# Mamba layer with routed experts on one core: the last state of batches 1 to 5 scaled by ScalarE behind the transposes, y in two parts

## The chip, the cores and the metric

One core of a Trainium2 chip. The metric is device time in microseconds of one execution. The engines are called by their names; in rows of the profile PE is TensorE, DVE is VectorE, ACT is ScalarE, POOL is GpSimd and SP is SyncE.

## The reference

x is 8 batches of 512 tokens of 128 features. After a layer norm (xn), two branches are added to x. The first is a Mamba block with 256 inner channels and 16 states:

```python
x_s, z = split(rmsnorm(xn) * norm_w @ in_proj_w.T)
u = silu(depthwise_conv4(x_s) + conv_b)
dt_raw, B, C = split(u @ x_proj_w.T)
delta = softplus(dt_raw @ dt_proj_w.T + dt_proj_b)
dA = exp(delta * A);  dBu = delta * u * B
h = dA_t * h + dBu_t            # over the 512 tokens, for each channel and state
y_t = sum over the 16 states of h * C_t
out = ((y + u * D) * silu(z)) @ out_proj_w.T + xn
```

The second routes each of the 4096 tokens to 2 of 8 experts (a gated FFN of inner width 352) and adds their weighted outputs.

## The kernel before, in words

The work goes by 8 batches b and, in each, by 16 states k; a pair is a step, numbered n = 16 b + k. Channels lie on partitions in two halves (hf = 0, 1), the 512 tokens along the free dimension, so one instruction handles 128 x 512 elements. Five engines run own instruction streams, each written out by hand in a function `step(b, k)` (`step0(k)` for batch 0), and they are tied by counting semaphores. There is no planner: what stands first in an engine's stream is done first.

One step in batches 1 to 5:
- ScalarE writes exp(delta * A_k) into a PSUM bank for each half (`decay_bank`, L554); two banks alternate.
- GpSimd computes dBu for both halves (`scaled`, L996) into one of two buffers; it may start when the scan two steps back has ended. It also issues the indirect loads of token rows (`load`, L980) and, spread over a batch, 11 elementwise products for the next batch's delta and gate.
- VectorE scans the tokens (`scan`, L1213) in place in the bank, then multiplies by C's row, which a DMA has spread over the partitions, into `h_sb` (`product`, L1232).
- TensorE transposes `h_sb` in 8 blocks of 128 x 128 and adds them up in PSUM banks 2 and 3 (`accumulate`, L1507), tokens now on partitions. The banks so hold the sum over the states.

State 0 of batches 1 to 5 is done otherwise (`BY_SCALAR`): the scan writes `h_sb` directly, there is no product, and ScalarE multiplies the transposed state in place in banks 2 and 3 by C's column (`multiplied`, L744: one value a partition, four copies of 128 x 256). It must be alone in the banks for that, so it is the first of a batch.

The end of a batch: after the transposes of state 15, ScalarE copies both banks to `y_sb` (`y_evac`, L761, in step 0 of the next batch), TensorE transposes this back with 8 transposes into the same banks (`y_turn`, L1603; they are called YB then), and VectorE multiplies by the gate (`gate`, L1240) into `g_sb`, which shares its memory with `y_sb`. Only then may state 0 of the next batch be transposed into the banks.

The 72 tiles of 128 routed tokens are laid over the steps from (1, 4) to (5, 11), one a step, in the gaps of all engines. In step g with tile j: TensorE does the down matmuls of tile j - 1 (L1672), the up matmuls of j (L1686), the gate matmuls of j + 1 (L1680) and the transpose of the rows of j + 2 (L1664). ScalarE does the output of j - 1 (`out_out`, L787), tanh of j + 1 (`gate_out`, L780) and the xT copy of j + 2 (`slots_out`, L769). VectorE does two products (L1259, L1266); the second waits for the up matmuls. Ahead of one another in TensorE's stream in step 0 of a batch stand: transposes of state 15, down, up, `y_turn`, gate matmuls, rows transpose, `rows` of a later batch (L1556), transposes of state 0; in step 1 down and up follow.

Batch 0 computes the routing beside its steps: `logits` (L1425), `choices` on VectorE, `totals` and `ranking` on TensorE with `totals_out` (L496) and `ranks_out` on ScalarE between them, one-hots on VectorE and `inverse` (L1455) on TensorE, and `sources` on VectorE (L1176 to L1181), from which GpSimd's loads take their indices. `keep` (L1411) is a matmul without use for its result. `by_vector` and `bank_read` translate "state m is done" into the semaphore and count to wait for:

```python
BY_SCALAR = [S * b for b in range(1, NB - 2)]
def by_vector(m):
    return m - sum(min(max(m - 2 * n, 0), 2) for n in BY_SCALAR)
def bank_read(eng, m):
    if m > 0 and (m - 1) // 2 in BY_SCALAR:
        wait(eng, "h_rdy", m)
    else:
        wait(eng, "p_rdy", by_vector(m))
```

## Time and profile before

| | |
|---|---|
| median of 3 runs | 606.79 us (605.84 to 608.28) |
| profiled execution, its own time | 606.02 us |
| its span, first to last instruction | 604.2 us |
| TensorE | 535.1 us busy, 3578 matmuls |
| VectorE | 581.3 us busy |
| ScalarE | 465.9 us busy |
| GpSimd | 489.8 us busy |
| mean granted TensorE clock | 0.980 |

The sum is made against the execution that the profile shows, 606.02 us. A row of a timeline is: start, duration, engine, line, operation, output and inputs, count of instructions merged, and in brackets the idle time before it with what ended it. Durations of merged rows are from the first start to the last end; the next group may start about 0.1 us before that. Step 0 of batch 3 begins with the scan at 262.53 us.

### The profile page before, as it was taken

The numbers are of one execution on the slowest core, as the hardware profiler recorded it, in microseconds if no ns is written. First come the engines' busy times: TensorE is split into PE (matmuls) and PEld (weight loads), VectorE is DVE, ScalarE is ACT, GpSimd is POOL, SyncE is SP. The second block draws the span as 40 slices with busy tenths as digits, with TensorE's granted clock in tenths as the row PEclk, the third lists the DMA queues.
The fourth block names the chain that finished last, engine by engine and source line by source line (L and its number), as shares of the span: only waits on it lengthen the run. The fifth ranks groups of instructions, "written<-read, shape, count | busy, mean of one in ns | idle before, by whom it ended". The sixth has DMA issues, their size and how long they took to land.

```text
span 604.2 us, 11465 instructions
## 1 busy us (share of the span) xinstructions
PE 535.1 (89%) x3578; PEld 419.5 (69%) x3578; DVE 581.3 (96%) x841; ACT 465.9 (77%) x952; POOL 489.8 (81%) x383
## 2 busy tenths in 40 slices
PE   5899889898898998999989999899989697778887
PEld 2377766647787878877887778877777465656564
DVE  6999989989999999999999999999999998999997
ACT  3899696369957998579876798768995589969880
POOL 3793466479999899998999889998997967885784
PEclk9899798989999999999999999999999999989999
DMA  7320229625787887889768888778874455233374
GB/s 200 148 91 2 74 60 282 226 84 184 237 314 237 311 277 222 292 244 339 262 189 305 276 305 275 243 257 274 284 264 157 156 219 197 103 100 108 79 143 87
DMA packets 61038, 122.48 MB, mean 203 GB/s; under 512 B 8362, under 2 KB 41778, under 8 KB 53938
## 3 DMA queue, kind: packets, MB, share of 16 engines
q1 hardware_dynamic: 53826, 112.42, 55.1%
q0 software_dynamic: 6144, 9.00, 6.6%
q10 hardware_dynamic: 1008, 0.33, 0.3%
q8 instruction: 29, 0.48, 0.3%
q14 instruction: 31, 0.25, 0.1%
HBM read 112.25 MB, written 9.47 MB: 201 GB/s over the span
## 4 chain that ended last, share of the span: by engine, by line
POOL 34%; PE 26%; DVE 15%; issue 14%; ACT 10%; DMA 1%; ACTq 0%; DVEq 0%; POOLq 0%; SPq 0%
POOL dbu L996 18%; POOL xs L980 6%; DVE bank L1213 6%; DVE h_sb L1232 5%; PE bank L1507 4%; PE bank L1541 3%; PE bank L1672 3%; ACT dbu L570 3%; PE bank L1686 2%; PE bank L1556 2%; ACT da L542 2%; PE bank L1564 2%; PE bank L1680 2%; POOL delta L463 2%; POOL sp_m L448 2%
## 5 line engine op out<-in xcount | busy, mean ns | idle before, releaser
L996 POOL TENSOR_TENSOR dbu<-du,xn_all 128x1024 f32<-128x1024 f32 x86 | 203.6, 2368 | 22.3 <-DVE bank L1213 13.7
L1213 DVE TENSOR_TENSOR_SCAN bank<-bank,dbu 128x512 f32<-128x512 f32 x160 | 195.2, 1222 | 1.0 <-ACT bank L554 0.7
L1232 DVE TENSOR_TENSOR h_sb<-bank,xh_all 128x512 f32<-128x512 f32 x230 | 152.5, 677 | 1.0
L1507 PE MATMUL bank<-id_sb,h_sb 128*128 128x128 f32 x992 | 132.5, 277 | 11.8 <-DVE h_sb L1232 9.3
L554 ACT ACTIVATE bank<-delta,a_sb 128x512 f32<-128x512 f32 x170 | 117.1, 691 | 27.5 <-DVE h_sb L1232 22.8
L1507 PEld LDWEIGHTS bank<-id_sb,h_sb 128*128 128x128 f32 x992 | 112.5, 143 | 26.5 <-DVE h_sb L1232 14.5
L1213 DVE TENSOR_TENSOR_SCAN bank<-da,bank 128x512 f32<-128x512 f32 x82 | 96.1, 1213 | 4.0 <-PE bank L1468 3.2
L1672 PEld LDWEIGHTS bank<-wd_sb,hid 117*128 117x128 f32 (+1 forms) x432 | 55.4, 190 | 42.8 <-issue 26.3
L980 POOL DMA_INDIRECT xs<-xn_rows,src x72 | 70.4, 978 | 12.8 <-issue 9.5
L1672 PE MATMUL bank<-wd_sb,hid 117*128 117x128 f32 (+1 forms) x432 | 62.9, 281 | 17.9 <-ACT xT L769 17.9
L570 ACT ACTIVATE dbu<-du_t,bc_sb 128x256 f32<-128x256 f32 x164 | 69.4, 497 | 5.8 <-PE bank L1468 3.4
L1468 PE MATMUL bank<-id_sb,dbu 128*128 128x128 f32 x328 | 51.6, 282 | 16.5 <-DVE h_sb L1232 9.1
L1541 PE MATMUL bank<-xhT,wk_sb 128*128 128x512 f32 x128 | 62.6, 617 | 1.4 <-ACT sp_m L866 0.8
L1468 PEld LDWEIGHTS bank<-id_sb,dbu 128*128 128x128 f32 x328 | 38.0, 144 | 37.2 <-issue 23.7
L542 ACT ACTIVATE da<-delta,a_sb 128x512 f32<-128x512 f32 x86 | 58.1, 713 | 4.8 <-DVE bank L1213 4.7
L1680 PE MATMUL bank<-xT,wgu_sb 128*118 128x128 f32 x432 | 59.0, 273 | 0.3 <-DVE ga L1259 0.3
L1686 PE MATMUL bank<-xT,wgu_sb 128*118 128x128 f32 x432 | 59.0, 272 | 0.0
L780 ACT ACTIVATE th<-bank 118x384 f32<-118x384 f32 x72 | 35.0, 485 | 29.1 <-PE bank L1680 28.3
L1046 POOL DMA_INDIRECT xhT<-y_slots,slot x40 | 38.7, 967 | 17.9 <-DVE bank L1213 7.1
L1686 PEld LDWEIGHTS bank<-xT,wgu_sb 128*118 128x118 f32 x432 | 52.7, 181 | 0.5 <-issue 0.5
L1680 PEld LDWEIGHTS bank<-xT,wgu_sb 128*118 128x118 f32 x432 | 52.4, 182 | 0.5 <-issue 0.5
L787 ACT ACTIVATE ys<-bank,stat 128x128 f32<-128x128 f32 x72 | 26.4, 366 | 24.8 <-PE bank L1672 24.3
(205 smaller groups left out, 906.8 us busy)
## 6 DMA issues: line engine op xcount, KB each, us to landing
xh_all<-b_rows SPq DMA_DIRECT2D x30, 1024.0 KB
xn_all<-b_rows SPq DMA_DIRECT2D x25, 1024.0 KB
wgu_sb<-in_w_gu SPq DMA_DIRECT2D x72, 352.0 KB, 4.2
wd_sb<-in_w_dn SPq DMA_DIRECT2D x72, 192.0 KB, 5.8
y_slots<-ys SPq DMA_DIRECT2D x72, 64.0 KB
xn_rows<-xn_all SPq DMA_DIRECT2D x2, 1040.0 KB, 10.2
out<-x_sb SPq DMA_DIRECT2D x7, 256.0 KB, 7.2
x_sb<-in_x SPq DMA_DIRECT2D x2, 640.0 KB, 5.9
```

The costliest lines, as they stand in the source:

```text
L554: nc.scalar.activation(bank_of(b, m)[:, :], delta[b % 2][:, hf, :], ACT.Exp, scale=a_sb[:, hf, k:k + 1]).then_inc(s["da_rdy"], 1)
L570: last = nc.scalar.activation(dbuT[k % 2][:, t, :], duT[:, t, :], ACT.Copy, scale=bc_sb[q][:, t, k:k + 1])
L980: nc.gpsimd.indirect_dma_start(xs[i][:, :], None, xn_rows, bass.IndirectOffsetOnAxis(ap=src[:, j:j + 1], axis=0)).then_inc(s[f"xs_in{i}"], 16)
L996: nc.gpsimd.tensor_tensor(dbu[k % 2][:, :, :], du[b % 2][:, :, :], b_ring[c % 2][:, k % CH, :].unsqueeze(1).to_broadcast([P, NH, T]), ALU. ...
L1213: nc.vector.tensor_tensor_scan(to, da_of(n)[:, hf, :] if n in IN_SBUF else at, inp, 0.0, ALU.mult, ALU.add).then_inc(s["h_rdy"], 1)
L1232: nc.vector.tensor_tensor(h_sb[k % 2][:, hf, :], bank_of(b, 2 * k + hf)[:, :], row, ALU.mult).then_inc(s["p_rdy"], 1)
L1468: last = nc.tensor.transpose(at[:, t * P:(t + 1) * P], dbuT[k % 2][:, t, hf * P:(hf + 1) * P], id_sb[:, :])
L1507: last = MM(HT[i][:, t % 2, hf * P:(hf + 1) * P], h_sb[k % 2][:, hf, t * P:(t + 1) * P], id_sb[:, :], is_transpose=True, start=(k == 0 and ...
L1541: last = MM(at[:, :], wk_sb[:, tap, hf * P:(hf + 1) * P], xhT[:, c, tap:tap + T], start=(tap == taps[0] if c == 0 else tap == 0), stop=(ta ...
L1672: last = MM(XD[:, P:P + H], hid[j % 2][0:FN[c], c * P:(c + 1) * P], wd_sb[j % NW][0:FN[c], c, :], start=(c == 0), stop=(c == NF - 1))
L1680: last = MM(GB[0:FW, c * P:(c + 1) * P], wgu_sb[j % NW][:, c * FS:c * FS + FW], xT[j % 2][:, :], start=True, stop=True)
L1686: last = MM(UB[0:FW, c * P:(c + 1) * P], wgu_sb[j % NW][:, F + c * FS:F + c * FS + FW], xT[j % 2][:, :], start=True, stop=True)
```

## The change

For batches 1 to 5 state 15 is treated like state 0: scan into `h_sb`, no product on VectorE. Since its C column is another than that of the sum in the banks, the sum of states 0 to 14 is first copied out by ScalarE (`summed_out`, in step 15), then the transposes of state 15 are written to the banks afresh (`start` set), and ScalarE copies them out with the scale of C's column (`spread`, four copies, in step 0 of the next batch). y so lies in two buffers (`da[1]`, `da[2]`, idle in batches 1 to 5), and `y_turn` adds both with 16 transposes. The gate waits for its half of y only. `own_columns` copies all 16 columns of C. In batch 0, the logits of batches 4 and 5 move one step later each (3 to 4, 4 to 5), one `keep` falls away, `totals_out` moves ahead of `vanishing(1, 1)` on ScalarE, y of batch 0 is turned ahead of `inverse(6)`, and `sources` moves from the end of step (1, 0) into step (1, 1), behind its first scan.

```diff
@@ near L152
+        parts_of = {b: [by_time(v) for v in ((da[1], da[2], da[0]) if b < 6 else (sp_m, sp_y, sp_e))] for b in range(NB - 1)}
+
+        def y_at(b):
+
+            if b in TRAILING:
+                return parts_of[b][0:1 + len(TRAILING[b])]
+            return [y_end if b == NB - 1 else parts_of[b][0] if 0 < b < 5 else y_sb]
+
+        def y_count(b):
+
+            return 2 * sum(len(y_at(b0)) for b0 in range(b))
@@ near L222
-        LOGITS_AT = {1: (3,), 3: (4,), 4: (5,), 6: (6, 7)}
+        LOGITS_AT = {1: (3,), 4: (4,), 5: (5,), 6: (6, 7)}
@@ near L241
-        BY_SCALAR = [S * b for b in range(1, NB - 2)]
+        LEADING = [S * b for b in range(1, NB - 2)]
+        TRAILING = {b: (S - 1,) for b in range(1, 6)}
+        BY_SCALAR = sorted(LEADING + [S * b + k for b, ks in TRAILING.items() for k in ks])
@@ ScalarE, step0
                 if k in (7, 8):
                     magnitudes(1, k - 7)
+                    if k == 8:
+                        totals_out()
                     vanishing(1, k - 7)
                 if k == 8:
-                    totals_out()
                     own_columns(1)
@@ ScalarE, step
-                if g - 1 in BY_SCALAR:
+                if 0 < b < 6:
+                    trailing(b, k)
+                if g - 1 in LEADING:
                     rows(b + 1)
                     multiplied(g - 1)
@@ ScalarE
-                nc.scalar.activation(bc_sb[c % 2][:, :, S:S + 1], at[:, 2 * P:3 * P].rearrange("p (t c) -> p t c", t=TT)[:, :, S:S + 1],
+                nc.scalar.activation(bc_sb[c % 2][:, :, S:2 * S], at[:, 2 * P:3 * P].rearrange("p (t c) -> p t c", t=TT)[:, :, S:2 * S],
                                      ACT.Copy).then_inc(s["cc_rdy"], 1)

             def y_evac(b):

+                if b in TRAILING:
+                    spread(b, S - 1)
+                    return
                 last = (b + 1) * S if b < NB - 1 else (NB - 1) * S + TURNED + 1
+                summed_out(last, y_at(b)[0])
+
+            def summed_out(last, at):
+
                 for i in range(2):
                     wait(act, "acc_mm", 2 * last - 1 + i)
-                    at = y_sb if b < NB - 1 else y_end
                     nc.scalar.activation(at[:, 2 * i:2 * i + 2, :], HT[i], ACT.Copy).then_inc(s["y_out"], 1)
+
+            def spread(b, k):
...
+                for i in range(2):
+                    act.wait_ge(s["acc_mm"], 2 * n + i + 1)
+                    for t in (2 * i, 2 * i + 1):
+                        last = nc.scalar.activation(at[:, t, :], HT[i][:, t % 2, :], ACT.Copy,
+                                                    scale=bc_sb[b % 2][:, t, S + k:S + k + 1])
+                    last.then_inc(s["y_out"], 1)
+
+            def trailing(b, k):
+
+                ks = TRAILING.get(b, ())
+                if k in ks and k == ks[0]:
...
+                    summed_out(b * S + k, y_at(b)[0])
@@ VectorE
             def gate(b):

                 wait(dve, "o_mm", b)
-                dve.wait_ge(s["yb_mm"], 2 * b + 2)
                 dve.wait_ge(s["z_rdy"], 2 * b + 2)
                 for hf in range(NH):
+                    dve.wait_ge(s["yb_mm"], 2 * b + (hf + 1 if b in TRAILING or 0 < b < 5 else 2))
@@ VectorE, step
+                if b == 1 and k == 1:
+                    sources()
                 product(b, k, 0)
...
-                if b == 1 and k == 0:
-                    sources()
@@ TensorE, accumulate
                 for i in range(2):
-                    if n - 1 in BY_SCALAR:
-                        pe.wait_ge(s["hc_rdy"], 2 * BY_SCALAR.index(n - 1) + i + 1)
+                    if n - 1 in LEADING:
+                        pe.wait_ge(s["hc_rdy"], 2 * LEADING.index(n - 1) + i + 1)
+                    if k in ks:
+                        pe.wait_ge(s["y_out"], y_count(b) + 2 * ks.index(k) + i + 1)
                     for t in (2 * i, 2 * i + 1):
                         for hf in range(NH):
                             last = MM(HT[i][:, t % 2, hf * P:(hf + 1) * P], h_sb[k % 2][:, hf, t * P:(t + 1) * P], id_sb[:, :],
-                                      is_transpose=True, start=(k == 0 and t % 2 == 0 and hf == 0), stop=(k == S - 1),
+                                      is_transpose=True, start=((k == 0 or k in ks) and t % 2 == 0 and hf == 0),
+                                      stop=(k == S - 1 or k + 1 in ks),
                                       skip_group_check=True)
@@ TensorE, y_turn
-                pe.wait_ge(s["y_out"], 2 * b + 2)
-                at = y_sb if b < NB - 1 else y_end
+                pe.wait_ge(s["y_out"], y_count(b + 1))
                 for hf in range(NH):
                     for t in range(TT):
-                        last = MM(YB[hf][:, t * P:(t + 1) * P], at[:, t, hf * P:(hf + 1) * P], id_sb[:, :], is_transpose=True,
-                                  start=(t == 0), stop=(b < NB - 1), skip_group_check=True)
+                        for i, at in enumerate(y_at(b)):
+                            last = MM(YB[hf][:, t * P:(t + 1) * P], at[:, t, hf * P:(hf + 1) * P], id_sb[:, :], is_transpose=True,
+                                      start=(t == 0 and i == 0), stop=(b < NB - 1 and i == len(y_at(b)) - 1), skip_group_check=True)
@@ TensorE, step0
-                if k in (0, 4):
+                if k == 0:
                     keep(LGB[:, 2 * C - 2 * H + 2 * E:])
@@ TensorE, step
                 if k == 0:
                     accumulate(g - 1)
                     if b == 1:
+                        y_turn(0)
                         inverse(6)
                         inverse(7)
...
-                if g in BY_SCALAR:
+                if g in LEADING and b > 1:
                     y_turn(b - 1)
```

How ScalarE's stream changes from step 15 of batch 1 to step 0 of batch 2 (the other middle batches are alike). Before, from the output of tile j - 1 in step 15 (`ys`; `bank<-delta` are the decays, `th` is tanh, `xT` the copy, `g_sb` the evacuation of y; the name ahead of a bracket is the semaphore waited for):

```order
L787 ACTIVATE ys<-bank,stat 128x128 [waits wt_rdy,ys_out0,dn_mm]
L554 ACTIVATE bank<-delta,a_sb 128x512 [waits delta_rdy,p_rdy]
L780 ACTIVATE th<-bank 118x384 [waits ga_rdy,g_mm]
L769 ACTIVATE xT<-bank 128x128 [waits u_mm,xt_mm]
L773 ACTIVATE stat<-xs,stat 128x1
L554 ACTIVATE bank<-delta,a_sb 128x512 [waits delta_rdy,p_rdy]
L761 ACTIVATE g_sb<-bank 128x512 [waits acc_mm] x2
L787 ACTIVATE ys<-bank,stat 128x128 [waits wt_rdy,ys_out1,dn_mm]
```

The same place in the changed kernel, whose line numbers differ:

```order
L785 ACTIVATE da<-bank 128x512 [waits acc_mm] x2
L836 ACTIVATE ys<-bank,stat 128x128 [waits wt_rdy,ys_out0,dn_mm]
L567 ACTIVATE bank<-delta,a_sb 128x512 [waits delta_rdy,h_rdy]
L829 ACTIVATE th<-bank 118x384 [waits ga_rdy,g_mm]
L818 ACTIVATE xT<-bank 128x128 [waits u_mm,xt_mm]
L822 ACTIVATE stat<-xs,stat 128x1
L567 ACTIVATE bank<-delta,a_sb 128x512 [waits delta_rdy,h_rdy]
L798 ACTIVATE da<-bank,bc_sb 128x256 [waits acc_mm,cc_rdy]
L798 ACTIVATE da<-bank,bc_sb 128x256
L798 ACTIVATE da<-bank,bc_sb 128x256 [waits acc_mm]
```

Two copies that wait for TensorE's transposes now stand ahead of everything else in step 15, and four copies stand where two stood.

TensorE's stream at the start of step 0 of batch 2, before (transposes of state 15, down, up, y, gate):

```order
L1507 MATMUL bank<-id_sb,h_sb 128x128 [waits p_rdy]
L1507 MATMUL bank<-id_sb,h_sb 128x128 x7
L1672 MATMUL bank<-wd_sb,hid 128x128 [waits xt_rdy,ys_rdy,hid_rdy]
L1672 MATMUL bank<-wd_sb,hid 128x128 x2
L1686 MATMUL bank<-xT,wgu_sb 118x128 [waits hid_rdy]
L1686 MATMUL bank<-xT,wgu_sb 118x128 x2
L1603 MATMUL bank<-id_sb,g_sb 128x128 [waits y_out]
L1603 MATMUL bank<-id_sb,g_sb 128x128 x7
L1680 MATMUL bank<-xT,wgu_sb 118x128 [waits ga_rdy,w_in1,xt_rdy]
```

And with the change:

```order
L1559 MATMUL bank<-id_sb,h_sb 128x128 [waits y_out,h_rdy]
L1559 MATMUL bank<-id_sb,h_sb 128x128 x3
L1559 MATMUL bank<-id_sb,h_sb 128x128 [waits y_out]
L1559 MATMUL bank<-id_sb,h_sb 128x128 x3
L1725 MATMUL bank<-wd_sb,hid 128x128 [waits xt_rdy,ys_rdy,hid_rdy]
L1725 MATMUL bank<-wd_sb,hid 128x128 x2
L1739 MATMUL bank<-xT,wgu_sb 118x128 [waits hid_rdy]
L1739 MATMUL bank<-xT,wgu_sb 118x128 x2
L1656 MATMUL bank<-id_sb,da 128x128 [waits y_out]
L1656 MATMUL bank<-id_sb,da 128x128 x15
L1733 MATMUL bank<-xT,wgu_sb 118x128 [waits ga_rdy,w_in1,xt_rdy]
```

The transposes of state 15 wait for ScalarE's copy of the sum and for the scan, no longer for a product, and y takes 16 transposes ahead of the gate matmuls.

## Rows read from the trace of the kernel before

**Rows 1.** The page, busy time of each engine, share of the span, instructions
```profile
PE 535.1 (89%) x3578; PEld 419.5 (69%) x3578; DVE 581.3 (96%) x841; ACT 465.9 (77%) x952; POOL 489.8 (81%) x383
```

**Rows 2.** Busy time by stretches; columns PE, PEld, DVE, ACT, POOL, PEclk, DMA share, GB/s
```profile
266.05:338.40 72.35, 67.21 (x507) 57.18 (x506) 71.55 (x99) 58.10 (x126) 67.08 (x44) 1.00 0.81 272
```

**Rows 3.** Chain of waits, 250 to 283 us: start, us, what
```profile
259.93 2.33 POOL dbu L996
...
277.80 0.67 PE bank L1686 x6
...
279.93 2.36 POOL dbu L996
```

**Rows 4.** Timeline of VectorE, boundary of batch 2 to 3
```profile
261.94 0.67 DVE L1232 TENSOR_TENSOR h_sb<-bank,xh_all 128x512 f32<-128x512 f32 x1
262.53 1.21 DVE L1213 TENSOR_TENSOR_SCAN h_sb<-bank,dbu 128x512 f32<-128x512 f32 x1
...
266.05 1.29 DVE L1240 TENSOR_TENSOR g_sb<-zs_sb,bank 128x512 f32<-128x512 f32 x2 [0.29 <-issue]
...
271.01 0.56 DVE L1266 TENSOR_TENSOR hid<-ga,bank 118x384 f32<-118x384 f32 x1 [0.35 <-issue]
```

**Rows 5.** Timeline of TensorE, the same boundary
```profile
260.12 1.04 PE L1507 MATMUL bank<-id_sb,h_sb 128*128 128x128 f32 x8
...
262.67 1.09 PE L1507 MATMUL bank<-id_sb,h_sb 128*128 128x128 f32 x8 [0.74 <-DVE h_sb L1232]
...
264.92 1.04 PE L1603 MATMUL bank<-id_sb,g_sb 128*128 128x128 f32 x8
265.80 0.82 PE L1680 MATMUL bank<-xT,wgu_sb 128*118 128x128 f32 x6
...
270.09 0.82 PE L1686 MATMUL bank<-xT,wgu_sb 128*118 128x128 f32 x6
```

**Rows 6.** Timeline of ScalarE, the same boundary
```profile
259.67 0.37 ACT L787 ACTIVATE ys<-bank,stat 128x128 f32<-128x128 f32 x1 [0.23 <-PE bank L1672]
260.46 0.69 ACT L554 ACTIVATE bank<-delta,a_sb 128x512 f32<-128x512 f32 x1 [0.43 <-DVE h_sb L1232]
261.85 0.49 ACT L780 ACTIVATE th<-bank 118x384 f32<-118x384 f32 x1 [0.70 <-PE bank L1680]
...
263.36 1.08 ACT L761 ACTIVATE g_sb<-bank 128x512 f32<-128x512 f32 x2
...
269.25 1.54 ACT L744 ACTIVATE bank<-bank,bc_sb 128x256 f32<-128x256 f32 x4
```

**Rows 7.** Timeline of GpSimd, step 4 of batch 2 (product for step 5)
```profile
207.62 2.36 POOL L996 TENSOR_TENSOR dbu<-du,xn_all 128x1024 f32<-128x1024 f32 x1 [0.82 <-DVE bank L1213]
```

**Rows 8.** Timelines of VectorE and GpSimd, boundary of batch 5 to 6
```profile
477.08 2.33 DVE L1213 TENSOR_TENSOR_SCAN bank<-bank,dbu 128x512 f32<-128x512 f32 x2
...
472.99 2.38 POOL L996 TENSOR_TENSOR dbu<-du,xn_all 128x1024 f32<-128x1024 f32 x1
```

**Rows 9.** Timelines of TensorE, VectorE, ScalarE, GpSimd: batch 0 and after
```profile
50.26 0.96 PE L1425 MATMUL bank<-wr_sb,xhT 128*128 128x8 f32 x8
...
51.81 1.23 DVE L1213 TENSOR_TENSOR_SCAN bank<-da,bank 128x512 f32<-128x512 f32 x1 [1.21 <-PE bank L1468]
...
80.81 2.34 DVE L1213 TENSOR_TENSOR_SCAN bank<-da,bank 128x512 f32<-128x512 f32 x2 [1.64 <-PE bank L1468]
...
76.69 0.63 ACT L828 ACTIVATE sp_y<-sp_y 128x512 f32<-128x512 f32 x1
77.22 0.15 ACT L496 ACTIVATE totc<-bank 128x2 f32<-128x2 f32 x1
...
125.25 1.20 POOL L980 DMA_INDIRECT xs<-xn_rows,src  x1 [1.57 <-DVE src L1179]
```

**Rows 10.** 120 to 122 us: busy time by stretch, and TensorE's timeline
```profile
120.00:122.00 2.00, 2.00 (x11) 1.70 (x9) 1.25 (x2) 1.38 (x2) 0.67 (x1) 0.50 0.00 0
...
120.22 1.88 PE L1603 MATMUL bank<-id_sb,g_sb 128*128 128x128 f32 x8
```

More of the change, by code:

```diff
@@ L597, in step0 @@
                     decay_bank(S, 0)
+                trailing(0, k)
                 if k == 3:
@@ L669, in step @@
                     decay_bank(g + 1, 1)
+                if b == 6:
+                    trailing(b, k)
                 if nxt is not None:
@@ L737, in multiplied @@
                 b, k = n // S, n % S
-                i0 = BY_SCALAR.index(n)
                 if 0 < b < 6:
@@ L1498, in accumulate @@
                     return
+                ks = TRAILING.get(b, ())
                 bank_read(pe, 2 * (n + 1))
@@ L1662, in slots_turn @@
                 if j == 0:
-                    pe.wait_ge(s["p_rdy"], 2 * S - 2)
+                    bank_read(pe, 2 * S - 2)
                 nc.tensor.transpose(XD[:, 0:P], xs[j % NXS][:, 0:H], id_sb[:, :]).then_inc(s["xt_mm"], 1)
@@ L1752, in step @@
                     y_turn(b)
-                if k > 0 and g - 1 not in BY_SCALAR:
+                if k > 0 and g - 1 not in LEADING:
                     accumulate(g - 1)
-                if g in BY_SCALAR:
+                if g in LEADING and b > 1:
                     y_turn(b - 1)
@@ L1766, in step @@
                     slots_turn(nn)
-                if k == 0 and g not in BY_SCALAR:
+                if k == 0 and g not in LEADING:
                     y_turn(b - 1)
@@ L1771, in step @@
                         rows(b + 1)
-                    if g in BY_SCALAR:
+                    if g in LEADING:
                         accumulate(g)
```

10 lines of the change are left out of this document (added).

## Prediction

> **What bounds the kernel now.** I read the page first, then the busy time by stretches, then the chain of waits, then the timelines of one batch boundary on four engines. The page shows VectorE busy for 96% of the span [rows 1], which says: take work off VectorE. The stretch from one gate to the next, which is one batch of the middle (its gates start 72.3 us apart), shows VectorE at 71.55 of 72.35 us, TensorE and GpSimd both at 67.1 [rows 2]. Three engines are nearly full, so what counts is where each is waited for. The chain of waits around the boundary from batch 2 to 3 is in [rows 3]: GpSimd's product for the first state of batch 3 ends at 259.93 + 2.33 = 262.26; then, from 262.67 to 278.47, the chain lies on TensorE without a gap; then a scan on VectorE lets GpSimd's next product start at 279.93, and from there GpSimd is back to back to the next boundary. So a batch has two parts: some 55 us where GpSimd decides and VectorE is only 0.2 us behind it, and some 17 us after the boundary where TensorE and ScalarE decide.
>
> What has to be seen in the timelines:
> - VectorE [rows 4]: the second product of state 15 starts at 261.94, the first scan of batch 3 at 262.53, 0.27 us after GpSimd's operand was there. So VectorE may reach this point earlier by 0.2 us, not by more. The gate waits 0.29 us, and the second FFN product at 271.01 waits 0.35 us: VectorE already waits for others here, before the change.
> - TensorE [rows 5]: transposes of state 14 at 260.12, of state 15 at 262.67 (0.74 us idle, for VectorE's product), y's 8 transposes at 264.92, the FFN gate matmuls at 265.80, and the up matmuls of the step after at 270.09 to 270.91, which the product at 271.01 waited for.
> - ScalarE [rows 6]: it does step 15's small work in the gaps, starts tanh at 261.85, evacuates y in 1.08 us from 263.36, and is done 0.48 us before TensorE takes it.
> - GpSimd [rows 7]: five steps into a batch it still waited 0.82 us for a scan, so a delay of VectorE before that point goes into the batch whole.
>
> **The change part by part.**
>
> *Ten products leave VectorE.* Two per boundary, at five boundaries. One costs 0.60 us from start to start (261.94 to 262.53) [rows 4], so 1.2 us per boundary, 6.0 us in all. At four of the five the next scan waits for GpSimd's 262.26, so they are worth 0.2 us each at most.
>
> *The sum of states 0 to 14 is copied out in step 15.* This is ScalarE's copy, new at this place and ahead of the last step's FFN output, the decay for the next batch, tanh and the xT copy. It waits for the transposes of state 14. TensorE makes these at 260.12 to 261.16 and not when the product is ready, because the matmuls ahead of them wait for ScalarE's copies of step 14. A half of the transposes is done some 0.7 us after their start, so the copy runs from 260.8 and, at 1.08 us for both halves, to 261.9. Before, ScalarE had issued the output (259.67, 0.37 us) and the decay (260.46, 0.69 us) by then. These now follow: 261.9 + 0.37 + 0.69, less 0.1 us of overlap, is 262.85, and tanh starts there and not at 261.85. **All of ScalarE behind it is 1.0 us later**, the wait of ScalarE being where the time goes, not its work. Queued behind it are the xT copy, which TensorE's down matmuls want, and the second decay.
>
> *State 15 is evacuated by four scaled copies.* The same form costs 1.54 us for four in [rows 6], against 1.08 us for the two copies: +0.46. Before, y was out at 264.44; now 264.44 + 1.0 + 0.46 = 265.9. TensorE's transposes of state 15 are ready long before (its scan ends 0.6 us earlier without the product between the halves, by 261.3 even if it starts late), so the 0.74 us idle there ends, but the engine then waits at y: **16 transposes start at 265.95 where 8 started at 264.92, 1.03 us later.** Eight cost 0.88 us start to start [rows 5], so the gate matmuls move from 265.80 by 1.03 + 0.87 = 1.9 us.
>
> *Behind y on TensorE* are the FFN gate matmuls, the xs transpose, the rows matmuls of the next batch, the transposes of state 0, down and up. All were back to back [rows 3]; none has a gap that could swallow 1.9 us. The up matmuls end at 272.8, and VectorE's product starts at 272.9 for 271.01. The gate by halves helps VectorE's first half only: its second half is ready at 265.95 + 1.74 + 0.2 = 267.9 and starts 1.3 us later than it did, well inside the delay that comes at 272.9. GpSimd's first scan-bound product afterwards is later by the same amount [rows 7]. So **each boundary costs 1.9 us, four of them (1 to 2, 2 to 3, 3 to 4, 4 to 5) 7.6 us.** Bounds: if ScalarE's wait is covered, only the 0.87 us of transposes stay, less 0.2 us: 2.7 us for four; if ScalarE's order holds TensorE's down matmuls up as well, by another 0.6 us each, 10 us.
>
> *The rule against this change.* The 8 transposes of y took 0.88 us, 0.11 us each, in this trace. The Trainium skill, "TensorE: Matmul & The Clock Gate", Part 4, has a 128x128 transpose at about 275 ns in one kernel's context, and says that transposes don't count as busy for the clock. By that figure the 32 added transposes would make +8.8 us of estimate instead of 3.5; the row decides, and the sum goes by it. The clock half of the rule is a rival below.
>
> *The last such boundary, 5 to 6*, has no FFN tiles. There the scan of batch 6 starts at 477.08, and GpSimd's operand was ready at 472.99 + 2.38 = 475.37 [rows 8]: 1.7 us of room. The two products go whole: -1.2 us.
>
> *Totals and logits.* The logits of batch 4 took 0.96 us of TensorE from 50.26, just ahead of the transposes that VectorE waited 1.21 us for: now behind them, -0.8 us (0.96 less the tail that the next matmuls overlap). The totals' copy stood behind an exponential on ScalarE (76.69 to 77.22, 0.53 us), TensorE's ranking behind it, and VectorE waited 1.64 us for what came after: -0.55 us [rows 9]. One keep-warm matmul fewer: nothing.
>
> *y of batch 0 ahead of the last inverse matmuls.* The 8 transposes stood at 120.22 behind the inverse matmuls, which waited for VectorE's one-hots. Now they run before; VectorE's gate, which waited for them, gains at most their 1.88 us [rows 10]. But the sources move behind a scan, and GpSimd's loads, which started at 125.25 on them, come 0.2 us later. Two products on, GpSimd no longer waits for VectorE's later scans and has made up about 0.6 us (an estimate from these two): I take -0.6; bounds -1.9 and +0.2 [rows 9].
>
> *C's columns in full instead of one*: the copy grows by 60 elements per partition, under 0.1 us where ScalarE has gaps: nothing.
>
> Sum: 7.6 - 1.2 - 0.8 - 0.55 - 0.6 = +4.4 us. The profiled execution took 606.0 us, 0.8 under the median 606.8; against the median the forecast is **611.2 us**. What a measurement of this kernel can tell from no change is about 0.5%, 3.0 us: the limits are 603.8 and 609.8.
>
> **The rivals.**
> - *Only the transposes count.* If ScalarE catches up (TensorE's state-14 transposes come earlier than in the trace, so the copy does not wait), four boundaries cost 0.7 us each: 2.8 - 3.2 = -0.4, that is 606.4 us. For: ScalarE idles 1.4 us in step 15. Against: that idling lies ahead of 260.8, the copy's start. Chance 0.22.
> - *GpSimd decides alone (faster).* If TensorE's chain after the boundary is hidden too, because y's transposes begin at 264.1, right behind the up matmuls, then each boundary gives the 0.2 us to GpSimd's 262.26: -0.8 - 3.2 = -4.0, 602.8 us. It decides if y is out before 264.1; by [rows 6] it is out at 265.9, so 1.8 us have to be wrong. Chance 0.12. If GpSimd didn't bound either, -6.0 - 2.0 would give 598.8: 0.03.
> - *The clock falls at the boundary.* TensorE now waits about a microsecond ahead of 16 transposes. In [rows 10] it was at 0.50, the 1.2 GHz level, after having idled for VectorE, and 8 transposes took 1.88 us for 1.04. Sixteen would take 1.7 us more, and the rows matmuls behind them about as much: 4 x 3.4 = +14, 625 us. Against: the clock was 1.00 in the middle batches [rows 2], with idle gaps of 0.74. It is by the skill's rule that transposes don't count, from the page named above, that this would happen. Chance 0.04.
>
> **How the numbers follow.** Forecast 0.59, 608 to 614 (the bounds above: four times 0.7 to 2.5 us less the gains of 2.0 to 3.5, the middle of it); transposes only 0.22; faster 0.15; clock 0.04. The likeliest gives 611.2. The range reaches down to the GpSimd case and up to the forecast's own bound: 603 to 614; left out are the two extremes and half of the GpSimd case. Slower by over 0.5%: most of the forecast and the clock case, 0.58. Same: the rest of it and the transposes-only case, 0.27. Faster: 0.15.
>
> **What would show it.** Right: in the boundary of batch 2 to 3, ScalarE idle over a microsecond ahead of its copy in step 15; TensorE idle about 1 us ahead of y's 16 transposes; VectorE waiting over a microsecond at its second FFN product of step 1; a gate-to-gate period of about 74.2 us for 72.3; VectorE's busy time down by 6 to 7 us while the span grows. Wrong: a period of 72.1 or less, or ScalarE's tanh of step 15 at its old distance from the first scan.

## The result, and the profile after

The changed kernel took **611.03 us**, the median of 6 runs (609.67 to 612.14), beside 606.52 us for 6 runs of the kernel before: ratio 1.0064, 95% interval 1.0046 to 1.0082. That is 2.8 to 5.0 us slower, where 4.4 was forecast. Its profiled execution took 611.24 us (span 609.4) against 606.02 (span 604.2), 5.2 us more.

The page of the changed kernel, busy time of each engine:

```profile
PE 543.2 (89%) x3616; PEld 425.2 (70%) x3616; DVE 576.1 (95%) x831; ACT 472.4 (78%) x972; POOL 489.4 (80%) x383
```

VectorE lost ten instructions and 5.2 us of busy time against [rows 1], TensorE gained 8.1 us and ScalarE 6.5, and GpSimd did the same work. The kernel with less work on its busiest engine is the slower one.

The stretch from one gate of the middle to the next in the changed kernel, in the columns of [rows 2]:

```profile
266.81:340.85 74.04, 68.45 (x514) 58.09 (x513) 70.49 (x96) 59.29 (x130) 67.06 (x43) 1.00 0.79 264
```

A batch takes 74.04 us for 72.35, with VectorE idle for 3.55 us of it (74.04 - 70.49) where it had been idle for 0.80. The granted clock is 1.00 as before.

The timeline of ScalarE in the changed kernel, boundary of batch 2 to 3, which answers to [rows 6] (start, us, what, idle time before it and what ended that):

```profile
260.69 1.08 ACT L785 ACTIVATE da<-bank 128x512 f32<-128x512 f32 x2 [1.33 <-PE bank L1559]
261.66 0.37 ACT L836 ACTIVATE ys<-bank,stat 128x128 f32<-128x128 f32 x1
261.91 0.70 ACT L567 ACTIVATE bank<-delta,a_sb 128x512 f32<-128x512 f32 x1
...
262.52 0.50 ACT L829 ACTIVATE th<-bank 118x384 f32<-118x384 f32 x1
...
263.94 1.59 ACT L798 ACTIVATE da<-bank,bc_sb 128x256 f32<-128x256 f32 x4
```

ScalarE stands still for 1.33 us ahead of its new copy. Behind it, in its queue, stand the FFN output and the decay, which wait for nothing of this copy (the experiment that puts the copy behind them shows both running in this gap), and then tanh; all three come 0.7 us or more later than in [rows 6]. The first scan of step 15 starts 0.07 us earlier here than before (258.10 for 258.17), so that 0.07 is added to each difference that follows: tanh is late by 262.52 + 0.07 - 261.85 = 0.74 us.

The timeline of TensorE in the changed kernel, the same boundary, which answers to [rows 5]:

```profile
260.05 1.04 PE L1559 MATMUL bank<-id_sb,h_sb 128*128 128x128 f32 x8
...
262.18 0.30 PE L1717 MATMUL bank<-id_sb,xs 128*128 128x128 f32 x1 [0.43 <-ACT ys L836]
262.31 1.05 PE L1559 MATMUL bank<-id_sb,h_sb 128*128 128x128 f32 x8
...
265.58 1.97 PE L1656 MATMUL bank<-id_sb,da 128*128 128x128 f32 x16 [0.69 <-ACT da L798]
267.39 0.82 PE L1733 MATMUL bank<-xT,wgu_sb 128*118 128x128 f32 x6
...
271.69 0.82 PE L1739 MATMUL bank<-xT,wgu_sb 128*118 128x128 f32 x6
```

The idle 0.74 us ahead of state 15's transposes is gone, as forecast, and 0.69 us has come ahead of y's. Those start 265.58 + 0.07 - 264.92 = 0.73 us late, and sixteen of them take 0.93 us more than eight took before the gate matmuls can start, which are 1.66 us late; so are the up matmuls, 1.67.

The timeline of VectorE in the changed kernel, the same boundary, which answers to [rows 4]:

```profile
262.65 1.22 DVE L1262 TENSOR_TENSOR_SCAN h_sb<-bank,dbu 128x512 f32<-128x512 f32 x1 [1.31 <-ACT bank L567]
...
266.81 1.46 DVE L1289 TENSOR_TENSOR g_sb<-zs_sb,bank 128x512 f32<-128x512 f32 x2 [0.92 <-issue]
...
272.60 0.56 DVE L1315 TENSOR_TENSOR hid<-ga,bank 118x384 f32<-118x384 f32 x1 [1.00 <-issue]
```

VectorE has 1.2 us less to do, and waits 1.31 us at once: for the decay of batch 3, which ScalarE issued behind its waiting copy. It then waits 0.92 us at the gate and 1.00 us at the second FFN product, which starts 1.66 us late. The time went into waits of VectorE for ScalarE and TensorE. (Where a row says `issue`, the view names no releaser; that the gate waited for y's transposes and the product for the up matmuls is read from TensorE's rows above.)

The page's shares of the chain that ended last, by engine, in the changed kernel:

```profile
PE 51%; ACT 19%; issue 15%; DVE 13%; POOL 1%; ACTq 1%; DVEq 0%; POOLq 0%
```

Before, this line began `POOL 34%; PE 26%; DVE 15%`. It suggests that the bound left GpSimd for TensorE; an experiment below shows how much that line may be trusted.

Where the 5.2 us lie, from the start of VectorE's first scan of each step in the two timelines (after less before; batch and step counted from 0):

| stretch | after less before, at its end | change in it | forecast |
|---|---|---|---|
| start to batch 0, step 2 | +1.27 | +1.27 | none |
| batch 0, step 2 to 12 (logits, totals) | -0.25 | -1.52 | -1.35 |
| to batch 1, step 15 (y of batch 0, sources) | -0.85 | -0.60 | -0.6 |
| to batch 2, step 2 (boundary 1 to 2) | -0.13 | +0.72 | +1.9 |
| to batch 5, step 2 (boundaries 2 to 5) | +5.04 | 3 x 1.72 | 3 x 1.9 |
| to batch 6, step 0 (boundary 5 to 6) | +3.48 | -1.56 | -1.2 |
| to batch 6, step 4 | +4.66 | +1.18 | none |
| to the last step | +5.23 | +0.56 | none |

The first row has no cause in the change; the section on what was not expected comes back to it.

### The profile page after: what moved, and what is told of

It is laid out like the page before. It is cut to its first block, busy times and chain, and to the rows that moved or that the text cites. A ratio compares the mean times of both kernels' runs of the same rounds, so it can differ in the third digit from the quotient of the medians.

```text
span 609.4 us, 11556 instructions
## 1 busy us (share of the span) xinstructions
PE 543.2 (89%) x3616; PEld 425.2 (70%) x3616; DVE 576.1 (95%) x831; ACT 472.4 (78%) x972; POOL 489.4 (80%) x383
## 4 chain that ended last, share of the span: by engine, by line
PE 51%; ACT 19%; issue 15%; DVE 13%; POOL 1%; ACTq 1%; DVEq 0%; POOLq 0%
PE bank L1559 9%; PE bank L1594 8%; PE bank L1725 8%; PE bank L1739 5%; PE bank L1733 5%; DVE h_sb L1281 5%; DVE bank L1262 4%; ACT bank L567 3%; ACT dbu L583 2%; ACT da L555 2%; PE bank L1617 2%; PE bank L1609 2%; PE bank L1517 2%; PE bank L1656 2%; PE bank L1693 1%
## 5 line engine op out<-in xcount | busy, mean ns | idle before, releaser
L1262 DVE TENSOR_TENSOR_SCAN bank<-bank,dbu 128x512 f32<-128x512 f32 x150 | 182.8, 1221 | 1.8 <-ACT bank L567 0.8
L1281 DVE TENSOR_TENSOR h_sb<-bank,xh_all 128x512 f32<-128x512 f32 x220 | 145.8, 678 | 0.8
```

The source lines that it names most:

```text
L1262: nc.vector.tensor_tensor_scan(to, da_of(n)[:, hf, :] if n in IN_SBUF else at, inp, 0.0, ALU.mult, ALU.add).then_inc(s["h_rdy"], 1)
L1281: nc.vector.tensor_tensor(h_sb[k % 2][:, hf, :], bank_of(b, 2 * k + hf)[:, :], row, ALU.mult).then_inc(s["p_rdy"], 1)
```

## The experiments

My theory was that each boundary costs 1.9 us, about half for ScalarE's wait and half for eight more transposes on a full TensorE. The rivals were that only the transposes count, that GpSimd hides all of it, and that the small moves of logits, totals, sources and y of batch 0 make the difference. The results, each with the distance from gate to gate in the middle (72.32 us before, 74.04 after):

| kernel | us, median | ratio to the kernel before, 95% interval | gate to gate |
|---|---|---|---|
| e1_rest_only | 605.05 | 0.9969 (0.9947 to 0.9990) | 72.37 |
| e10_rest_again | 605.17 | 0.9978 (0.9959 to 0.9997) | 72.36 |
| e2_trailing_only | 612.40 | 1.0075 (1.0050 to 1.0100) | 74.04 |
| e3_copy_after_decay | 607.44 | 1.0010 (0.9992 to 1.0028) | 73.28 |
| e4_eight_turns | 606.25 | 0.9993 (0.9973 to 1.0013) | 73.14 |
| e6_y_behind_gate | 608.94 | 1.0019 (0.9992 to 1.0047) | 73.71 |
| e5_both_moves | 606.66 | 0.9975 (0.9952 to 0.9998) | 72.93 |
| e9_y_between | 605.58 | 0.9971 (0.9958 to 0.9984) | 72.61 |
| e8_free_removal | 601.47 | 0.9912 (0.9891 to 0.9933) | 71.85 |
| e7_only_batch5 | 604.51 | 0.9957 (0.9942 to 0.9972) | 72.36 |

### The small moves alone

```diff
-        TRAILING = {b: (S - 1,) for b in range(1, 6)}
+        TRAILING = {}
```

> The change without its main part: TRAILING is empty, so state 15 has its product on VectorE again; totals, logits, y of batch 0, sources, the gate by halves and the buffers stay. Theory A (the time is lost at the four boundaries with FFN tiles, on ScalarE and TensorE): no boundary cost is left, only the gains of batch 0 and its end, so 605.5 us give or take 0.8, and gates 72.3 us apart in the middle batches. Rival B (the small moves cost time, the products' removal gains): above 611.

Measured: 605.05 us, and 72.37 us from gate to gate. The shift against before is -1.76 us at step 2 of batch 3, -1.70 at batch 4, -1.65 at batch 5: the middle costs nothing once state 15 goes the old way. The slower time is all in the trailing state, and the small moves are worth about 2 us.

### The trailing state alone

```diff
-        LOGITS_AT = {1: (3,), 4: (4,), 5: (5,), 6: (6, 7)}
+        LOGITS_AT = {1: (3,), 3: (4,), 4: (5,), 6: (6, 7)}
...
-                    if k == 8:
-                        totals_out()
                     vanishing(1, k - 7)
                 if k == 8:
+                    totals_out()
...
-                if g in LEADING and b > 1:
+                if g in LEADING:
                     y_turn(b - 1)
```

(The sources, y of batch 0 and the keep-warm matmul go back in the same way.)

> The main part alone: logits, the keep-warm matmul, totals, y of batch 0 and sources are back where they were before. Theory A: 606.5 plus 5.4 (0.7 at boundary 1 to 2, three times 1.7, less 0.4 at 5 to 6) is 611.9 us, gates 74.0 us apart. Rival B: 604 or less. If the first boundary was cheaper only because batch 1 ended early against GpSimd, it costs 0.7 here too, since GpSimd limits step 14 of batch 1 with or without the gain.

Measured: 612.40 us and 74.04 from gate to gate. With the kernel above this splits the change: +5.1 us (612.4 - 607.3, the runs of before beside it) and -2.25 (605.05 - 607.3). The two sum to 2.85, less than the 4.5 of the change itself; the intervals, over a microsecond to either side of each, allow that, and the split is a rough one. The expectation missed at the first boundary: batch 1 to 2 cost 1.61 us here, nearly as the others did, and not 0.7. So its cheapness in the changed kernel comes from the small moves. The timeline of the changed kernel, late in batch 1 and at that boundary, all engines:

```profile
179.97 1.23 DVE L1262 TENSOR_TENSOR_SCAN bank<-bank,dbu 128x512 f32<-128x512 f32 x1 [0.31 <-POOL dbu L1045]
...
185.00 1.22 DVE L1262 TENSOR_TENSOR_SCAN h_sb<-bank,dbu 128x512 f32<-128x512 f32 x1
186.02 1.04 PE L1559 MATMUL bank<-id_sb,h_sb 128*128 128x128 f32 x8
```

VectorE had come early into batch 1 and was held there by GpSimd, 0.9 us in all (-1.74 at step 8, -0.85 at step 14). TensorE was not: it turned state 14 at 186.02, 1.02 us after VectorE's scan of step 15, where at the boundary of batch 2 to 3 the same two rows are 1.95 us apart (258.10 and 260.05). ScalarE's copy had its operand 0.93 us sooner after VectorE's scan; it still stood idle for 1.32 us ahead of it, and TensorE for 0.69 us ahead of y, as at the other boundaries.

### ScalarE's copy behind the decay

```diff
-                if 0 < b < 6:
-                    trailing(b, k)
                 if g - 1 in LEADING:
...
                     decay_bank(g + 1, 0)
+                    if b:
+                        trailing(b, k)
```

> The changed kernel with ScalarE's copy of the sum of states 0 to 14 behind the FFN output and the first decay of the next batch, instead of ahead of them; the same work. Theory A: ScalarE fills its wait for TensorE's transposes with these two, so y is out 0.8 to 0.9 us earlier and each of the three full boundaries costs 0.9 instead of 1.7: 608.3 us, gates 73.2 us apart, and VectorE's wait of 1.2 us for the decay is gone. Rival C (only the 8 added transposes count, ScalarE's order is hidden): 611, no change, 74.0 us.

Measured: 607.44 us and 73.28; 608.3 and 73.2 were expected. ScalarE's and VectorE's rows of this kernel's timeline, boundary of batch 2 to 3:

```profile
258.44 0.69 ACT L567 ACTIVATE bank<-delta,a_sb 128x512 f32<-128x512 f32 x1
259.27 1.09 ACT L785 ACTIVATE da<-bank 128x512 f32<-128x512 f32 x2
260.36 0.49 ACT L829 ACTIVATE th<-bank 118x384 f32<-118x384 f32 x1
260.85 1.22 DVE L1262 TENSOR_TENSOR_SCAN h_sb<-bank,dbu 128x512 f32<-128x512 f32 x1 [0.93 <-POOL dbu L1045]
```

The copy has no wait over 0.2 us in front of it any more, and VectorE's wait for the decay is gone. But the scan waits 0.93 us all the same, now for GpSimd. The order of two pieces of work on ScalarE was worth 74.04 - 73.28 = 0.76 us a boundary.

### Eight transposes of y in place of sixteen

```diff
-                        for i, at in enumerate(y_at(b)):
+                        for i, at in enumerate(y_at(b)[0:1]):
...
-                                      start=(t == 0 and i == 0), stop=(b < NB - 1 and i == len(y_at(b)) - 1), skip_group_check=True)
+                                      start=(t == 0 and i == 0), stop=(b < NB - 1), skip_group_check=True)
```

> The changed kernel with y turned back by 8 transposes and not 16: state 15 is left out of y in batches 1 to 5, all the rest (scan, transposes, four scaled copies, waits) is done. Theory A: TensorE's chain behind y is 0.87 us shorter at each of three boundaries and by less at the first: 608.2 us, gates 73.2 us apart. If the transposes are covered: 611, 74.0 us.

Measured: 606.25 us and 73.14 from gate to gate, so the eight cost 74.04 - 73.14 = 0.90 us a boundary, 3.6 for four. The price per boundary was right (0.87). The total was expected 2 us higher, with three boundaries in full; by the period the fourth, the first one, gains 0.83 too, and the rest, about a microsecond, is not accounted for. The row of TensorE in this kernel's timeline, boundary of batch 2 to 3:

```profile
264.48 1.09 PE L1656 MATMUL bank<-id_sb,da 128*128 128x128 f32 x8 [0.69 <-ACT da L798]
```

The wait ahead of y stays at 0.69 us: it is ScalarE's, and does not depend on how much TensorE has to do. The two prices, 0.76 and 0.90, sum to 1.66 of the 1.72 us.

### TensorE's order

Two runs take y's transposes from ahead of TensorE's FFN gate matmuls to behind these and the xs transpose; one with ScalarE's order of the change, one with that of the experiment before the last.

```diff
-                if g in LEADING and b > 1:
-                    y_turn(b - 1)
                 if g + 1 in BY_PE:
...
                 if nn is not None:
                     slots_turn(nn)
+                if g in LEADING and b > 1:
+                    y_turn(b - 1)
```

> Only TensorE's move: y's transposes behind the gate matmuls and the rows transpose, ScalarE's copy where the change has it. Theory A: the 0.7 us that TensorE idles ahead of y is filled, so 0.7 us per boundary come back, three times: 609.0 us, gates 73.3 us apart. If ScalarE's lateness alone decides: 611, 74.0 us.

> The copy of the sum behind the decay on ScalarE, and on TensorE y's 16 transposes behind the FFN gate matmuls and the rows transpose of the next tile. Theory A: TensorE's wait for y is filled with 0.8 us of work that did not need y, so both costs go; y's transposes start at about the same distance as before and end 0.1 us late against the before order: 605.0 to 606.0 us, gates 72.3 to 72.5 us apart, GpSimd setting the pace. Rival D (VectorE's later gate, at the end of y's transposes, then holds the next scan): 607.5 or more, 73 us apart.

Measured: 608.94 us and 73.71 with TensorE's move alone (609.0 and 73.3 expected, so the total agrees and the period does not); 606.66 and 72.93 with both (605 to 606 and 72.3 to 72.5 expected). TensorE's gap ahead of y is filled, and yet the period falls by less than expected. TensorE and VectorE in the run with both moves, boundary of batch 3 to 4:

```profile
340.69 0.88 PE L1733 MATMUL bank<-xT,wgu_sb 128*118 128x128 f32 x6
...
341.83 0.30 PE L1717 MATMUL bank<-id_sb,xs 128*128 128x128 f32 x1 [0.25 <-ACT ys L836]
341.97 1.91 PE L1656 MATMUL bank<-id_sb,da 128*128 128x128 f32 x16
...
343.14 1.46 DVE L1289 TENSOR_TENSOR g_sb<-zs_sb,bank 128x512 f32<-128x512 f32 x2 [1.01 <-PE bank L1656]
```

The xs transpose waits for ScalarE's FFN output, which stands behind the four scaled copies, and y now stands behind that wait; the gate waits 1.01 us, where it waited 0.55 us with ScalarE's move alone (boundary of batch 2 to 3). So the next run, again with ScalarE's copy behind the decay, put y right behind the gate matmuls and ahead of the xs transpose:

```diff
                 if nxt is not None:
                     gate(nxt)
+                if g in LEADING and b > 1:
+                    y_turn(b - 1)
```

> As e5_both_moves, with y's transposes behind the gate matmuls and ahead of the rows transpose, which in e5 held them for ScalarE's FFN output. Theory A: y's transposes start 0.4 us earlier than in e5, so gates 72.5 us apart instead of 72.9, and 605.5 us. If the rows transpose's wait for ScalarE then only moves behind y and holds the chain there: 72.9, 606.7 us.

Measured: 605.58 us and 72.61. TensorE and VectorE in this run, boundary of batch 2 to 3:

```profile
263.59 0.89 PE L1733 MATMUL bank<-xT,wgu_sb 128*118 128x128 f32 x6
264.36 1.97 PE L1656 MATMUL bank<-id_sb,da 128*128 128x128 f32 x16
265.59 1.46 DVE L1289 TENSOR_TENSOR g_sb<-zs_sb,bank 128x512 f32<-128x512 f32 x2 [0.57 <-PE bank L1656]
```

TensorE has no gap left here, and the boundary costs 72.61 - 72.37 = 0.24 us more than without the trailing state. TensorE's order, with ScalarE's already mended, was so worth 73.28 - 72.61 = 0.67 us a boundary. The work of the change, with two groups of instructions moved, is about 5.5 us faster than the change (0.9971 against 1.0064, each to its own runs of before). It still does not beat the kernel that has only the small moves.

### VectorE's ten products for nothing

This run takes the products away and adds no work on ScalarE or TensorE; state 15 goes into y unscaled.

```diff
-        TRAILING = {b: (S - 1,) for b in range(1, 6)}
-        BY_SCALAR = sorted(LEADING + [S * b + k for b, ks in TRAILING.items() for k in ks])
+        TRAILING = {}
+        BY_SCALAR = sorted(LEADING + [S * b + S - 1 for b in range(1, 6)])
```

> As e1_rest_only, and in batches 1 to 5 the scan of state 15 writes into h_sb without a product: the ten products are gone and nothing stands in their place (state 15 goes into y unscaled, by the same 8 transposes, so the multiplication with C of this state is left out). Theory A (GpSimd binds at the boundary): scan 0 of a middle batch waits 0.9 us for GpSimd's product, the gates are 72.0 to 72.1 us apart instead of 72.37, and only 5 to 6 gives up to 1.2 us: 603 us. Rival E (VectorE is the bound, each product counts): 1.2 us per batch, 71.2 us apart, 599 us.

Measured: 601.47 us and 71.85 from gate to gate ((407.42 - 263.73) / 2). VectorE's scan that opens batch 4, in this kernel's timeline:

```profile
332.35 1.23 DVE L1262 TENSOR_TENSOR_SCAN h_sb<-bank,dbu 128x512 f32<-128x512 f32 x1 [0.89 <-POOL dbu L1045]
```

Of the 1.2 us taken from VectorE, 72.37 - 71.85 = 0.5 us a boundary come out of the period; VectorE waits 0.89 us for GpSimd's product where the two products had been. With GpSimd's work as it is, that is the most that this change could win in the middle, 2 us for four, before it pays for anything. It is more than the 0.2 us that the prediction allowed. This kernel also warns of the chain's shares, its page's line being:

```profile
PE 51%; ACT 17%; issue 15%; DVE 15%; POOL 1%; ACTq 1%; DVEq 0%; POOLq 0%
```

It is nearly the line of the changed kernel, in a kernel that is 1.5% faster than it (0.9912 against 1.0064) and that has the products' removal held up by GpSimd. Where three engines end within tenths of a microsecond of each other, these shares say little of which one sets the pace.

### Only where there is room

The last edit turns state 15 of batch 5 alone by TensorE, with ScalarE's copy behind the decay, and keeps the small moves.

```diff
-        TRAILING = {b: (S - 1,) for b in range(1, 6)}
+        TRAILING = {5: (S - 1,)}
```

> The small moves, and the trailing state on ScalarE in batch 5 alone, where no FFN tiles run at the end. Theory A: e1_rest_only's time less the 0.4 us that was left of the boundary 5 to 6 in the changed kernel, 604.6 us, gates 72.4 us apart. Rival: what VectorE gains there (1.5 us at scan 0 of batch 6) is wholly given back by step 4 of batch 6, 605.0.

> e1_rest_only once more, with more rounds and beside e7 and e9: 605.1 us, gates 72.4 us apart, the profile's start of batch 1 earlier than before by 0.9 to 1.8 us.

Measured: 604.51 us, ratio 0.9957 (0.9942 to 0.9972), against 0.9978 (0.9959 to 0.9997) for the small moves alone on the same chip. It is the fastest of the complete kernels, and beats both the kernel before and the changed one. That it beats the small moves alone, by 0.7 us, is likely but not settled by these intervals. VectorE's rows in its timeline, around the start of batch 6:

```profile
471.65 2.33 DVE L1262 TENSOR_TENSOR_SCAN h_sb<-bank,dbu 128x512 f32<-128x512 f32 x2
473.90 2.54 DVE L1262 TENSOR_TENSOR_SCAN bank<-bank,dbu 128x512 f32<-128x512 f32 x2
...
477.94 1.46 DVE L1289 TENSOR_TENSOR g_sb<-zs_sb,bank 128x512 f32<-128x512 f32 x2 [0.33 <-PE bank L1656]
```

From the last scans of batch 5 to the first of batch 6 it is 2.25 us, where the kernel before took 3.80 (its scan of step 15 started at 473.28, the next at 477.08, [rows 8]) and the small moves alone 3.79: 1.54 us won. The gate then waits 0.33 us. From step 15 of batch 5 to step 4 of batch 6 this kernel gains 0.75 us on the kernel before, at the same granted clock of 1.00. (The small moves alone lose 0.6 there, at a lower granted clock: see below.)

## Why the prediction was right, and where its steps were off

**The mechanism held.** ScalarE idles ahead of its copy (1.33 us, over a microsecond as named), TensorE takes y late, the rest of TensorE's queue follows without a gap, VectorE waits at the second FFN product, and the period is 74.04 us for a forecast 74.2. Three of the signs came out smaller than they were named: TensorE idle for 0.69 us ahead of y and not about 1, VectorE idle for 1.00 us at the FFN product and not over 1, and its busy time down by 5.2 us and not by 6 to 7. The order experiment and the eight-transposes experiment price the halves separately and they add up, which none of the rivals allows.

**The boundary, 1.9 us forecast, 1.72 measured.** The transposes were right: 0.87 forecast, 0.90 by experiment. The other half was mis-sized, 1.03 forecast and 0.76 by experiment. The step at fault is "261.9 + 0.37 + 0.69, less 0.1 us of overlap". It added durations, but ScalarE starts one instruction before the last has ended: from the copy's start to tanh's it took 1.83 us (260.69 to 262.52), not 2.04, and the copy started at 260.69 for 260.8. All of ScalarE behind it is then 0.7 us late and not 1.0.

**The first boundary, 0.72 us for 1.9.** The step at fault is to have priced four boundaries alike. The change moves all engines forward in batch 1, GpSimd then holds VectorE by 0.9 us and not TensorE, and so the chain through TensorE and ScalarE, which is as long as elsewhere, starts earlier against VectorE. That the small moves do this is shown by the run without them (1.61 us); the chain of reasons between is read from the rows above, not tried.

**A wait that the text did not name.** The prediction had the decay late with everything else on ScalarE and followed only what TensorE made of that. The scan that opens the next batch waits for the decay too, 1.31 us, and this swallows all that the products had freed before GpSimd has any say. The sum did not suffer, since by [rows 3] the pace after the boundary is TensorE's.

**Boundary 5 to 6, -1.2 forecast.** At the boundary -1.56 us came, as there is room ahead of GpSimd. But 1.18 of it was gone four steps later. VectorE's and TensorE's rows of the changed kernel there:

```profile
483.08 1.97 PE L1656 MATMUL bank<-id_sb,da 128*128 128x128 f32 x16 [1.28 <-ACT da L798]
...
484.31 1.46 DVE L1289 TENSOR_TENSOR g_sb<-zs_sb,bank 128x512 f32<-128x512 f32 x2 [0.25 <-PE bank L1656]
...
493.24 0.60 PE L1517 MATMUL bank<-id_sb,dbu 128*128 128x128 f32 x4
...
494.63 1.23 DVE L1262 TENSOR_TENSOR_SCAN bank<-da,bank 128x512 f32<-128x512 f32 x1 [0.71 <-PE bank L1517]
```

Two things were lost. The gate waits 0.25 us for y's sixteen transposes and its second half waits again inside the row (1.46 us long for 1.27): 0.50 us by the next step. The prediction did not count y there, and the step at fault is "the two products go whole": the room was measured against GpSimd and not against y behind it. Then a scan waits 0.71 us, by the view for TensorE's transposes of dbu (in batch 6 ScalarE computes part of dbu and TensorE turns it), though these are recorded as done at 493.24 + 0.60 = 493.84, 0.79 us before the scan: another 0.68 us. This second loss looks like one of this execution. The kernel with the trailing state alone has the same code there and TensorE's rows at the same distances, and its two scans run on without a wait:

```profile
494.81 2.48 DVE L1261 TENSOR_TENSOR_SCAN bank<-da,bank 128x512 f32<-128x512 f32 x2
```

It wins 1.05 us at the boundary (7.15 us behind the kernel before in step 15 of batch 5, 6.10 in step 4 of batch 6), near the 1.2 forecast. What held the scan in the changed kernel's profile is open.

**TensorE's clock in batches 6 and 7.** The kernel with the small moves alone loses 0.61 us from step 0 to step 4 of batch 6 (-1.66 to -1.05), for another reason. TensorE's rows there, and its busy time by stretches in the columns of [rows 2]:

```profile
477.39 1.50 PE L1656 MATMUL bank<-id_sb,g_sb 128*128 128x128 f32 x8 [0.74 <-ACT g_sb L785]
...
475.42:491.24 15.82, 14.94 (x78) 9.90 (x78) 15.24 (x19) 11.45 (x22) 13.29 (x10) 0.89 0.44 163
```

and the same of the kernel before:

```profile
479.05 1.09 PE L1603 MATMUL bank<-id_sb,g_sb 128*128 128x128 f32 x8 [0.74 <-ACT g_sb L761]
...
477.08:492.29 15.21, 13.41 (x78) 8.96 (x78) 15.14 (x20) 11.46 (x22) 12.89 (x10) 1.00 0.46 169
```

The code there is the same, TensorE's last idle times before it are the same (1.63 us ahead of state 15's transposes, 0.74 ahead of y's), and y's eight transposes took 1.50 us for 1.09: for part of this stretch the granted clock was 0.50, the 1.2 GHz level. The repeat of this kernel has the same clock, 0.89, and the same loss, 0.60. The changed kernel had 1.00 there, and does not share this loss.

The 0.56 us that both the changed kernel and the small moves alone lose in batch 7 go with the clock too. From step 0 to step 4 of batch 7, before and in the changed kernel:

```profile
538.86:554.48 15.62, 12.83 (x84) 10.75 (x83) 14.99 (x19) 14.98 (x31) 10.22 (x9) 0.90 0.32 102
543.53:559.71 16.18, 13.86 (x83) 11.85 (x82) 15.11 (x20) 15.08 (x31) 10.22 (x9) 0.79 0.29 97
```

All twelve profiles of this document sort in this way. Where the mean clock of this stretch is 0.90 to 0.93 (the kernel before, the products for nothing, TensorE's move alone, batch 5 alone) it lasts 15.3 to 15.6 us; where it is 0.79 to 0.83 (the eight others) it lasts 16.1 to 16.5. No run changed the clock by itself, so this is read and not tried, and why one kernel gets the lower clock and another does not is open. It is no part of the work that the change moves.

**Totals and logits, and y of batch 0.** Together -1.35 and -0.6 were forecast, and -1.52 and -0.60 stand in the profile. That close a match is partly luck. The stretch of the first gave -2.9 us in the profile of the small moves alone, and -2.6 in its repeat; and of the second, 1.49 us were won by step 2 of batch 1 and 0.89 given back to GpSimd by step 14.

**Errors that cancelled.** The boundaries were forecast 1.7 us too dear (7.6 for 0.72 + 3 x 1.72 = 5.88), and batches 5 to 7 some 1.4 us too cheap (-1.2 for -1.56 + 1.18 + 0.56 = +0.18). A late start of the profiled execution, +1.27 us, makes up for most of the rest. The boundary's mechanism and size were forecast; that the total came within 0.2 us of 611.2 is luck in part.

**The rivals.** "Only the transposes count" falls: without the eight, 0.82 us a boundary is left over the kernel before. "GpSimd decides alone" falls: y is out at 263.94 + 1.59 = 265.53, long after 264.1. GpSimd does bound what can be won, at 0.5 us. The clock did not fall. Busy time by stretches in the changed kernel, from y's transposes on, in the columns of [rows 2]:

```profile
265.58:267.50 1.92, 1.92 (x18) 1.92 (x19) 1.00 (x2) 0.79 (x2) 1.74 (x3) 1.00 0.69 243
267.50:270.00 2.50, 2.50 (x12) 0.96 (x10) 2.41 (x5) 1.51 (x4) 2.34 (x2) 1.00 0.79 141
```

It was 1.00, the 2.4 GHz level, through the sixteen transposes and behind them, after idle times of 0.43 and 0.69 us. The rule of the Trainium skill, "TensorE: Matmul & The Clock Gate", Part 4, that a transpose doesn't count as busy in the same way for the clock, cost nothing at this boundary. Its figure of about 275 ns for a 128x128 transpose agrees with the recorded length of a single one here, 0.27 us for the xs transpose:

```profile
268.04 0.27 PE L1717 MATMUL bank<-id_sb,xs 128*128 128x128 f32 x1
```

But that is not what one costs in a row of them: sixteen took 1.97 us from the first start to the last end, and eight more cost 0.90, 0.11 each.

## What to carry to other kernels

Work taken from the busiest engine is worth only what the next engine in line leaves of it (0.5 of 1.2 us here), so measure that first, by a kernel in which the work just vanishes. Price a moved wait by what is queued behind it in order: an instruction that waits belongs behind everything that is ready, and on ScalarE as on TensorE that alone was worth 0.76 and 0.67 us a boundary. Where a program repeats a boundary, use the cheaper form only at those repeats whose neighbours have room, and look some steps further for where the gain is given back.

## What the runs showed that I had not expected

- The same code starts differently from execution to execution. In batch 0 the six 512-column matmuls below are the same in both kernels. TensorE's row in the timeline of the kernel before:

```profile
29.11 3.19 PE L1541 MATMUL bank<-xhT,wk_sb 128*128 128x512 f32 x6
```

and in that of the changed kernel:

```profile
29.45 4.00 PE L1594 MATMUL bank<-xhT,wk_sb 128*128 128x512 f32 x6
```

  They took 0.81 us more, and most of the profiled execution's +1.27 us at the start follows from this and from the 0.34 us by which they began late. TensorE's granted clock differs. Over these two rows, before and after, in the columns of [rows 2]:

```profile
29.11:32.30 3.19, 3.19 (x10) 1.47 (x9) 3.05 (x5) 3.14 (x7) 3.19 (x4) 0.86 0.58 238
29.45:33.45 4.00, 4.00 (x10) 1.74 (x9) 3.86 (x6) 3.13 (x7) 4.00 (x5) 0.68 0.32 131
```

  From 22 to 42 us the mean clock was 0.91 in the kernel before and in the repeat of the small moves, which is at -0.03 us at step 2 of batch 0, and 0.74 or 0.75 in the changed kernel and six others, which are at +0.97 to +1.26 us there. The small moves alone were run twice, and stand once on either side: this is scatter, and no effect of an edit. (Of the other three, one had 0.83 and is at +0.40, and two were some 2 us late already at the first scan, which is open.) The execution profiled of the run with both moves took 611.2 us beside a median of 606.66. One profile is no measure of a kernel's total here; the distance from gate to gate repeats to 0.01 us in the pair of equal kernels (72.37 and 72.36).
- A gate in two halves on one line took 1.46 us in the kernels that turn y by sixteen transposes and 1.27 to 1.29 with eight, so the second half waited some 0.17 us inside the row, and no wait is printed for it.
- The chain's shares by engine (GpSimd 34% before, 1% after) turned over with tenths of a microsecond, and were alike in the changed kernel and in one 1.5% faster.
